# Reordering one step of a software pipeline on TensorE, ScalarE and VectorE in a fused LoRA and FFN kernel

## The reference, cut to what matters

```python
# layer 1: linear map plus routed low-rank experts
base   = x @ W.T
logits = x @ Wr.T + one_hot(language_id) * 5.0       # 8 experts, top 2, softmax over the two
lora   = einsum(x @ A_e.T, gates, B_e)               # 8 experts of rank 16
y      = base + 2.0 * lora
# layer 2: masked linear map
dots      = softmax(y @ centroids.T / 0.1)           # 64 centroids
hits      = dots > 0.01
query_sel = any(hits, over centroids)                # per token
row_sel   = any(hits, over tokens)[assignments]      # per output feature
out       = x + where(query_sel & row_sel, y @ weight.T + bias, 0)
```

## Time and profile before

| | us |
|---|---|
| median of 3 runs (lowest, highest) | 338.72 (338.47, 339.54) |
| the profiled execution's own time | 339.44 |
| its span | 337.6 |
| TensorE busy | 330.6 (98%) |
| VectorE busy | 260.6 (77%) |
| ScalarE busy | 139.7 (41%) |

### The profile page before, as it was taken

The page is one execution under the profiler, slowest core; times in us unless marked ns, Lnnn a source line. Parts: engine busy times, 40 slices in busy tenths (PEclk is TensorE's granted clock), DMA queues, the critical chain, the costliest instruction groups (busy, mean ns, idle before and its releaser), DMA issues.

```text
span 337.6 us, 4608 instructions
## 1 busy us (share of the span) xinstructions
PE 330.6 (98%) x1758; PEld 290.2 (86%) x1758; DVE 260.6 (77%) x469; ACT 139.7 (41%) x234; POOL 1.0 (0%) x9
## 2 busy tenths in 40 slices
PE   8999999999999999999899999999999999999995
PEld 7888889999999999999677888888888888888885
DVE  3837966568898889889896979769398594993967
ACT  5824746445656655655533314222223331231220
POOL 1000000000000000000000000000000000000000
PEclk9999999999999999999999999999999999999999
DMA  7965451333534343336603181814607237051113
GB/s 237 417 192 188 153 188 63 124 127 124 182 107 136 139 126 124 126 103 229 232 9 117 68 292 48 289 51 162 214 1 277 98 128 245 0 196 55 62 64 124
DMA packets 14358, 49.10 MB, mean 145 GB/s; under 512 B 1728, under 2 KB 1984, under 8 KB 14336
## 3 DMA queue, kind: packets, MB, share of 16 engines
q1 hardware_dynamic: 14336, 48.80, 41.4%
HBM read 40.41 MB, written 8.39 MB: 145 GB/s over the span
## 4 chain that ended last, share of the span: by engine, by line
PE 86%; DVE 11%; issue 1%; ACT 0%; POOL 0%; POOLq 0%; DVEq 0%
PE ps L965 23%; PE ps L966 22%; PE ps L967 22%; PE ps L974 7%; PE ps L1032 7%; PE ps L1034 3%; DVE gop_lo L602 2%; DVE gop_raw L605 2%; DVE xt_lo L602 1%; PE ps L971 1%; DVE s_raw L605 1%; DVE u L934 0%; PE ps L1043 0%; DVE u L860 0%; DVE hits L754 0%
## 5 line engine op out<-in xcount | busy, mean ns | idle before, releaser
L965 PE MATMUL ps<-vt_hi,w_hi 128*128 128x288 f32 (+1 forms) x184 | 58.7, 319 | 0.0
L967 PE MATMUL ps<-vt_hi,w_lo 128*128 128x288 f32 (+1 forms) x184 | 58.0, 315 | 0.0
L966 PE MATMUL ps<-vt_lo,w_hi 128*128 128x288 f32 (+1 forms) x184 | 58.0, 315 | 0.0
L407 ACT ACTIVATE u<-ps 128x512 f32<-128x512 f32 x32 | 19.1, 597 | 84.1 <-PE ps L967 57.5
L966 PE MATMUL ps<-gop_lo,sl_s_hi 128*128 128x512 f32 x128 | 49.8, 389 | 0.0
L1032 PE MATMUL ps<-aw,xt_hi 128*128 128x400 f32 x128 | 39.0, 366 | 0.4 <-DVE xt_lo L602 0.4
L965 PE MATMUL ps<-gop_hi_t,sl_s_hi 128*128 128x512 f32 x96 | 37.4, 390 | 0.0
L967 PE MATMUL ps<-gop_hi_t,sl_s_lo 128*128 128x512 f32 x96 | 37.3, 389 | 0.0
L966 PEld LDWEIGHTS ps<-vt_lo,w_hi 128*128 128x128 f32 x184 | 34.6, 188 | 1.6
L965 PEld LDWEIGHTS ps<-vt_hi,w_hi 128*128 128x128 f32 x184 | 34.5, 188 | 1.6
L967 PEld LDWEIGHTS ps<-vt_hi,w_lo 128*128 128x128 f32 x184 | 34.5, 188 | 1.6
(11 more groups left out here) (135 smaller groups left out, 662.3 us busy)
## 6 DMA issues: line engine op xcount, KB each, us to landing
xt_raw<-in_xt SPq DMA_DIRECT2D x32, 512.0 KB, 4.0
nat<-in_x SPq DMA_DIRECT2D x16, 512.0 KB, 4.0
out<-nat SPq DMA_DIRECT2D x15, 512.0 KB, 2.7
w_raw<-in_w SPq DMA_DIRECT2D x8, 512.0 KB, 3.3
wraw<-in_w SPq DMA_DIRECT2D x6, 512.0 KB, 4.2
vt_raw<-in_v SPq DMA_DIRECT2D x4, 576.0 KB, 5.7
vt_raw<-in_v SPq DMA_DIRECT2D x4, 256.0 KB, 4.7
wq_raw<-in_wq SPq DMA_DIRECT2D x4, 256.0 KB, 4.9
```

What stands on the lines that cost most here:

```text
L407: return nc.scalar.activation(dst, src, ACT.Copy)
L965: nc.tensor.matmul(dst, l_hi, r_hi, start=start, stop=False, skip_group_check=True)
L966: nc.tensor.matmul(dst, l_hi, r_lo, start=False, stop=False, skip_group_check=True)
L967: return nc.tensor.matmul(dst, l_lo, r_hi, start=False, stop=stop, skip_group_check=True)
```

## The change

Three lists are reordered; no instruction is added, removed or resized. TensorE: both chunks come first, then `turn_hg`, token product 0, `lora_logits`, token product 1. DVE: `route` comes ahead of `split_x(0, n)`, `split_x(1, n)` ahead of `split_hgt`, and in even steps `r_rest` goes behind `split_w`. ACT: `take_rest` comes ahead of `split_x(0, n)`, `router_exp` directly behind it and so ahead of `r_part` or `t_part`, and `evict(n, 1)` ahead of `keep_hgt` and `split_w`. SP's list is not edited.

```diff
@@ ScalarE @@
             for n in range(NPAIR):
                 if n >= 1:
+                    take_rest(n - 1)
                     split_x(0, n)
-                    take_rest(n - 1)
+                    router_exp(n - 1)
                     if n >= 2 and n % 2 == 0:
                         r_part(n // 2 - 1, slice(A1, HALF), chunk_number(n - 1, 1))
                     elif n >= 2:
                         t_part(n // 2 - 1)
-                    router_exp(n - 1)
                 evict(n, 0)
                 if n >= 1:
                     split_x(1, n)
+                evict(n, 1)
+                if n >= 1:
                     keep_hgt(n - 1)
                     split_w(n + KG + 1)
-                evict(n, 1)
-                if n >= 1:
                     softmax_exp(n - 1)
@@ VectorE @@
             for n in range(1, NPAIR):
+                route(n - 1)
                 split_x(0, n)
-                route(n - 1)
                 jj = n // 2 - 1
                 if n >= 2 and n % 2 == 0:
                     t_sums(KH + jj, jj, slice(A1, HALF), chunk_number(n - 1, 1))
-                    r_rest(KH + jj, jj, slice(A1, HALF))
                 elif n >= 2:
                     t_rest(jj)
+                split_x(1, n)
                 split_hgt(n - 1)
-                split_x(1, n)
                 split_w(n + KG + 1)
+                if n >= 2 and n % 2 == 0:
+                    r_rest(KH + jj, jj, slice(A1, HALF))
                 softmax_max(n - 1)
                 softmax_hits(n - 1)
@@ TensorE @@
             for n in range(NPAIR):
                 chunk(n, 0)
-                token_product(0, n)
+                chunk(n, 1)
                 if n >= 1:
                     turn_hg(n - 1)
-                chunk(n, 1)
+                token_product(0, n)
                 if n >= 1:
                     lora_logits(n - 1)
                 token_product(1, n)
```

## The result

| | before | after |
|---|---|---|
| median of 12 runs, us | 338.81 | 340.48 |
| lowest, highest | 338.47, 339.85 | 339.80, 341.17 |
| profiled execution, own time (span) | 339.44 (337.6) | 340.63 (338.8) |

The ratio after to before is 1.0041, 95% interval 1.003 to 1.0051: the kernel is 1.4 us slower (the medians differ by 1.7). I had forecast 338.6 us and no measurable change, with 340.2 as the upper end.

A forecast was written before the change was run, and what follows sets the result against it. DVE's chain of fixed work up to 163 us was taken as the bound, with TensorE nearly full. Terms of -0.05, -0.3 and +0.2 us gave -0.15 us, so 338.6 us from 338.72, range 337.5 to 340.2.

The forecast's parts named there:

- What bounds the kernel: Second sweep: DVE's fixed chain from 76.24 to 163 us sets when stage 3 goes on, not TensorE.
- TensorE's order: Logits begin at 8.83 instead of 8.93 us into the step, step length unchanged; gain 0.05 us in step 1.
- that exchange costs the end nothing: PE stalls of 0.1 to 0.4 us in odd steps replace even-step stalls of 0.2; slack over 1.4 us at 163.14.
- `r_rest` away from `t_sums`: DVE, steps 2, 4 and 6: the split moved between them saves 0.1 us a step, 0.3 us in all.
- ACT's other edits: take_rest first, r_part and t_part behind router_exp, evict(n, 1) 2.5 us earlier; none comes last, cost 0.
- my sum: DVE's chain: -0.05 - 0.3 + 0.2 = -0.15 us, from the median of 338.72 us.
- The wait that gets closer: den on DVE needs router_exp, queued on ACT behind a later tile 0 load; late landings cost 0.2 us over seven loads.
- The W load close behind tile 0's load: DMA: W's load now follows tile 0's at once; the second of a pair pays, the load in front isn't delayed.
- the second rival: DVE's den waits for router_exp behind tile 0 loads, made 4.3 us by W's load: +1.55 us, 340.3; chance 0.18.
- The first rival: TensorE is the bound; its stalls and the gap ahead of 163.14 us go, 2.2 us: 336.5; chance 0.12.
- theory P: Follow-up runs: PE sets the time and its own waits ahead of lora_logits, 2.0 us in the profile, are the loss.

The follow-up runs named there:

- e11: Kernel before, with only r_rest moved between softmax_max and softmax_hits on DVE in even steps; ratio 0.9972 to the kernel before.
- e9: Kernel before, with the next step's split_x(0) (rest_a(0) in step 7) between softmax_max and softmax_hits on DVE, ACT's copies moved to match; ratio 0.9949, median 337.39 us.
- e4: Changed kernel, with split_hgt ahead of split_x(1, n) on DVE in odd steps only; ratio 1.0022 to the kernel before.
- e1: Changed kernel, with split_w ahead of evict(n, 1) on ACT; ratio 1.0009 to the kernel before.
- e2: Changed kernel, with router_exp ahead of split_x(0, n) on ACT; ratio 1.0023 to the kernel before.
- e3: Changed kernel, with split_w ahead of evict(n, 1) and router_exp ahead of split_x(0, n) on ACT; ratio 0.9987 to the kernel before.
- e6: e3 plus r_rest or t_rest between softmax_max and softmax_hits in steps 2 to 6, t_sums there in step 7; ratio 1.0012 to the kernel before.
- e10: e3 plus r_rest between softmax_max and softmax_hits on DVE in even steps only; ratio 0.9978 to the kernel before.
- e7: Kernel before, with PE's new list alone, ACT's and DVE's lists as before; ratio 1.0088 to the kernel before, from four runs.

## Why the prediction was wrong

- *What bounds the kernel.* Right. e11 gains by a move on DVE alone, e9 by moves on DVE and ACT, both with PE's list untouched, and the loss after is DVE's 1.5 us.
- *TensorE's order.* Half right. `lora_logits` begins 8.93 us into step 1 as before, and PE stood there in the three odd steps, 0.45 and 0.44 us in steps 5 and 7 (forecast 0.1 to 0.4) and 1.1 in step 3 behind the late load. But "that exchange costs the end nothing" was wrong. The waits put the next turn 0.45 us later against DVE's step, and without them (e4) DVE doesn't wait for `w_hi`.
- *`r_rest` away from `t_sums`.* Right, 0.12 us a step. That agrees with the earlier trace rows, and not with the rule that the Trainium skill, page "VectorE: DVE Perf Modes", section "The DRAIN you can't avoid", gives first: that the next instruction doesn't start until the pipe is empty.
- *ACT's other edits, "none of these comes last. Cost 0."* This step failed. I had checked that `evict(n, 1)` and `r_part` are early enough for their users, but not what is queued behind the moved turn on ACT. `split_w` stands behind `keep_hgt`, `keep_hgt` behind the turn, and the turn went from 5.5 to 6.4 us into the step. In even steps DVE comes to `w_lo` first, as it has neither `t_rest` nor `r_rest` ahead of it any more. The term was 0.41 us in each of three steps, 1.2 us in all; e1 measured 1.1. With it my sum gives 338.72 - 0.15 + 1.2, 339.8 us, and with the late load's 0.6 us (next point) in place of 0.2, 340.2; measured were 340.48.
- *The wait that gets closer.* The mechanism was right, the value too small. The margin in step 3 was put at 3.9 to 4.3 us of landing time; the load took 5.3 and cost 0.6, for which I had 0.2 over all steps. e2 measured 0.6. That a late landing would hit the same step in profile after profile was not foreseen (below).
- *The W load close behind tile 0's load.* Right. In the profile of the changed kernel the load in front landed in 3.1 to 3.4 us for seven of the eight tile 0 loads of the sweep, and W behind it in 4.1 or more. So the second rival's condition (all of them 4.3) did not hold. That its 340.3 us lies close to the 340.48 measured is luck: only the one late load in step 3, 0.6 us, came by its road, and 1.2 us came by `w_hi`.
- *The first rival*, PE as the bound, had forecast 336.5 us and is ruled out by the result itself. In the form of theory P it had 1.002 for e3 and 0.998 for e4, and measured were 0.9987 and 1.0022; e9 sped the kernel up by a wait that isn't PE's.

## What to carry to other kernels

When an event moves later in a step (here the turn), follow what is queued behind each engine's wait for it, not only the users of the moved instructions: an in-order engine hands the delay on to unrelated work such as the next weights. When two engines are both nearly full, look for the one whose idle time is a wait inside its own chain, and fill that gap with work that the next step wants first and that isn't much longer than the gap. Here fills of 0.97 and 1.14 us in a gap of 0.84 gained. One of 2.29 us turned the gap into a loop over both engines and gained nothing.

## What the runs showed of the hardware

The late landing of step 3 comes back at the same place in one profile after the other. In the changed kernel the load of tile 0 issued at 86.94 us took 5.3 us. In its four variants e1 to e4 the load issued between 86.3 and 87.1 us took 5.0 to 5.9, in e6 and e10 5.4 and 4.9. The DMA view of the changed kernel for that load, and for 88 to 89 us (queue, packets, MB, share):

```profile
xt_raw<-in_xt SPq DMA_DIRECT2D x1, 512.0 KB, 5.3
...
q8 instruction: 1, 0.02, 9.0%
```

One packet of an instruction queue, 0.02 MB, was on a DMA engine while the load was in flight. In the kernel before, the one load of 5.5 us, issued at 119 us, has such a packet in 121 to 123 us:

```profile
xt_raw<-in_xt SPq DMA_DIRECT2D x1, 512.0 KB, 5.5
...
q8 instruction: 1, 0.02, 4.8%
```

The loads issued before and behind it, from 107 to 135 us, landed in 3.1 to 3.3 us. One run comes near to a test: in e7, which also has PE's new order, such a packet lies in 85 to 86 us, ahead of the load issued at 87.23 us, and that load took 3.3 us. But in the changed kernel packets at 103, 127 and 139 us lie in loads that took only 3.8 to 4.3. That the packet delays the load, and why by 2 us at this place, is read from coincidences; no run was made to move it, so it is not shown.
